# Opening of a graph-and-attention kernel: splitting the normalised input straight from PSUM

## What is computed

```python
x = x + gnn(layernorm(x), [src, dst], ...)      # two SAGE layers
x = x + ffn(layernorm(x), ...)                  # router, three attentions, MLP

def sage_conv(x, edge_index, W_l, b_l, W_r):
    src, dst = edge_index
    agg = segment_sum(x[src], dst) / max(segment_sum(1, dst), 1)[:, None]
    return agg @ W_l.T + b_l + x @ W_r.T
h = relu(sage_conv(x, edge_index, W1_l, b1, W1_r))
gnn = sage_conv(h, edge_index, W2_l, b2, W2_r)
```

## Time and profile before

| | us |
|---|---|
| median of 3 runs (lowest to highest) | 1723.16 (1722.98 to 1728.6) |
| the profiled execution, its time | 1724.62 |
| the profiled execution, its span | 1722.8 |
| PE busy | 1595.9 (93%) |
| DVE busy | 1140.0 (66%) |
| ACT busy | 872.8 (51%) |
| POOL busy | 744.8 (43%) |

### The profile page before, as it was taken

One profiled execution on the slowest core, in us unless ns is written; L12 is line 12 of the kernel. 1 busy time (PEld: TensorE's weight loads), 2 busy tenths in 40 slices (PEclk: granted clock), 3 DMA queues, 4 the chain that ended last, 5 costly groups with the idle time before them and its releaser, 6 DMA issues.

```text
span 1722.8 us, 26353 instructions
## 1 busy us (share of the span) xinstructions
PE 1595.9 (93%) x9714; PEld 1354.1 (79%) x9714; DVE 1140.0 (66%) x1810; ACT 872.8 (51%) x1733; POOL 744.8 (43%) x608
## 2 busy tenths in 40 slices
PE   2788999699999999999999998999999997899997
PEld 1467977588788888878789997878888885678876
DVE  7898735730788888840288885168898885843323
ACT  3796313321688878731177772158878872301100
POOL 3220222135436446133568773453545565632330
PEclk9999999799999999999999999999999998899999
DMA  3000011243021112042222304302111210110111
GB/s 101 18 26 2 26 55 55 83 178 72 8 54 31 31 31 56 7 184 69 60 60 61 71 9 150 90 1 57 34 31 31 73 49 19 38 37 25 49 37 59
DMA packets 37352, 91.62 MB, mean 53 GB/s; under 512 B 6462, under 2 KB 8980, under 8 KB 36717
## 3 DMA queue, kind: packets, MB, share of 16 engines
q1 hardware_dynamic: 37229, 89.99, 18.9%
HBM read 45.40 MB, written 13.86 MB: 34 GB/s over the span
## 4 chain that ended last, share of the span: by engine, by line
PE 78%; DVE 10%; ACT 6%; issue 3%; POOL 2%; DMA 1%; DVEq 0%; SPq 0%; ACTq 0%; POOLq 0%
PE ps L1088 14%; PE ps L1069 13%; PE ps L761 10%; PE ps L762 10%; PE ps L763 10%; PE ps L1054 8%; PE ps L1055 6%; ACT F L1355 1%; PE ps L1013 1%; PE ps L1014 1%; PE ps L1104 1%; ACT F L1364 1%; ACT F L1261 1%; PE ps L948 1%; ACT R L1274 1%
## 5 line engine op out<-in xcount | busy, mean ns | idle before, releaser
L1274 ACT ACTIVATE R<-ps 125x500 fp32r<-125x500 f32 (+3 forms) x632 | 291.7, 508 | 146.6 <-PE ps L1069 145.2
L1854 DVE TENSOR_REDUCE TB<-ps 125x1 f32<-125x1250 f32 (+4 forms) x240 | 299.5, 1262 | 82.1 <-PE ps L1055 56.5
L595 POOL TENSOR_TENSOR w_hi<-w_raw,zero 128x512 fp32r<-128x512 f32 x92 | 107.0, 1163 | 560.5 <-PE ps L763 281.5
L1863 DVE TENSOR_TENSOR R<-ps,R 125x500 fp32r<-125x500 f32 (+3 forms) x632 | 323.9, 568 | 12.9 <-ACT R L1274 12.9
L1261 ACT ACTIVATE F<-ps,TB 125x1250 f32<-125x1250 f32 (+4 forms) x240 | 275.9, 1156 | 60.2 <-DVE TB L1854 60.2
L1088 PE MATMUL ps<-R 125*128 125x252 f32 (+1 forms) x2080 | 288.9, 286 | 2.3 <-DVE F L1906 2.3
L1069 PE MATMUL ps<-ident,F 125*125 125x125 f32 x2040 | 260.0, 275 | 9.6 <-ACT F L1261 8.5
L1088 PEld LDWEIGHTS ps<-R 125*128 125x128 f32 x2080 | 256.1, 189 | 2.6 <-DVE R L1863 1.6
L1069 PEld LDWEIGHTS ps<-ident,F 125*125 125x125 f32 x2040 | 239.5, 189 | 13.1 <-ACT F L1261 12.7
L1054 PE MATMUL ps<-R 128*125 128x512 f32 (+5 forms) x624 | 240.1, 385 | 4.9 <-DVE R L1863 3.8
L761 PE MATMUL ps<-R,w_hi 128*128 128x512 f32 (+3 forms) x576 | 212.8, 370 | 17.8 <-POOL w_lo L610 11.2
(11 more groups left out here) (209 smaller groups left out, 2418.3 us busy)
## 6 DMA issues: line engine op xcount, KB each, us to landing
R<-F SPq DMA_DIRECT2D x96, 312.5 KB, 5.3
w_raw<-in_weights SPq DMA_DIRECT2D x88, 256.0 KB, 2.6
F<-in_weights SPq DMA_DIRECT2D x3, 1024.0 KB, 8.4
x_d<-F SPq DMA_DIRECT2D x10, 250.0 KB
zt_d<-F SPq DMA_DIRECT2D x1, 2500.0 KB, 14.0
F<-zt_d SPq DMA_DIRECT2D x1, 2500.0 KB, 9.2
xt_d<-F SPq DMA_DIRECT2D x4, 625.0 KB, 3.1
qc_d<-F SPq DMA_DIRECT2D x4, 625.0 KB, 5.6
```

The lines of the kernel that those rows point to most:

```text
L595: return eng.tensor_tensor(to, a, zero[0:to.shape[0], :].to_broadcast(list(to.shape)), ALU.add)
L1274: eng.activation(probs_run(K, n, 0, part, lo, hi), ps[0:P, 3 * (n % 2) + bank, P * (lo - j0):P * (hi - j0)] .rearrange("p (c t) -> p c t", ...
L1854: ins = eng.tensor_reduce(out=ngm[0:P, 2 * (n % 2) + part:2 * (n % 2) + part + 1], in_=flat(n % 2)[0:P, at:at + P * blocks], op=ALU.max, a ...
L1863: eng.tensor_tensor(probs_run(K, n, 1, part, lo, hi), ps[0:P, 3 * (n % 2) + bank, P * (lo - j0):P * (hi - j0)] .rearrange("p (c t) -> p c ...
```

## The change

- ACT copies each transposed tile from PSUM straight into the high part of `X0` (125 columns of each of the four blocks), and DVE subtracts it from PSUM straight into the low part, tile by tile, inside the normalising loop. The copy to `ZT`, `cut_hi` and `cut_lo` of `x` go, and with them the semaphore `sp["x"].lo`. `ln0.ev`, which frees the PSUM bank, is now counted up by DVE. PE waits for all ten tiles after its first group of the graph loop.
- The tile number of a source node is computed with three instructions (scale and shift, add 1.5 * 2^23, subtract it again, which rounds) in place of nine.
- POOL waits for these before it zeroes the 7580 columns, and zeroes the other 5120 in two halves, of which the first waits for the first five tiles. DVE waits for `at_zero` (now 4) ahead of its first `add_group`, no longer ahead of the loop.
- SP loads the weight units 0 and 1 behind `x` and ahead of the write at L474, units 2 and 3 behind the bias row, and then the five small constants.
- ACT runs one square root on a constant ahead of its first work.

```diff
--- before.py
+++ after.py
@@ -36,6 +36,7 @@
 WK = WD * NT
 TA = T + WD
 LAG = 2
+ROUND = 1.5 * 2 ** 23
 EPS = 1e-5
 SCALE = float(HD) ** -0.5
 BANK = 512
@@ -243,6 +244,7 @@
         mr1 = sb("mr1", [128, NT, 2])
         rcnt = sb("rcnt", [128, NT, 1])
         rt = sb("rt", [128, 48])
+        spare = rt[:, 6:7]
         b1g = rt[:, 40:44]
         bq_add = rt[:, 44:48]
         eps_t = sb("eps_t", [128, 1])
@@ -392,7 +394,7 @@
         comp = Sems(sem, "comp", "in_ row hi lo ps ev st")
         deg = Sems(sem, "deg", "lk sum ps free inv mem")
         sp = {n: Sems(sem, "cut_" + n, names) for n, names in
-              dict(x="hi lo", h="hi lo", s="val hi lo", os="hi lo", t="val hi lo st0 st1", ot="hi lo", oc="hi lo",
+              dict(x="hi", h="hi lo", s="val hi lo", os="hi lo", t="val hi lo st0 st1", ot="hi lo", oc="hi lo",
                    m="hi lo").items()}
         pj = {n: Sems(sem, "prod_" + n, names) for n, names in
               dict(g="ps a v", qk="a", v="ps v", u="a v t", uc="ps v", m1="a v t", m2="ps a v").items()}
@@ -464,12 +466,7 @@
             eng.dma_start(d_i, dst.rearrange("(q r) -> q r", q=EQ)).then_inc(e.in_, 16)
             for n, (lo, hi) in enumerate(X_LOADS):
                 eng.dma_start(XA[0:P, lo:hi, :], x[lo:hi, :, :].rearrange("i p f -> p i f")).then_inc(x_in[n], 16)
-            eng.dma_start(lncol[:], ln_cols[:, 0:6, :]).then_inc(small_in, 16)
-            eng.dma_start(b1g, ln_cols[:, 6, :]).then_inc(small_in, 16)
-            eng.dma_start(b1col[:], mlp_b1).then_inc(small_in, 16)
-            eng.dma_start(rt[:, 0:1], router_b1).then_inc(small_in, 16)
-            eng.dma_start(rt[0:1, 8:16], router_b2).then_inc(small_in, 16)
-
+            load_units(0, 2, G0)
             eng.wait_ge(e.mm, 2)
             eng.dma_start(mm_d.rearrange("m (q j) -> q m j", j=EJ), mm2.rearrange("q (m j) -> q m j", m=2)
                           ).then_inc(e.mmd, 16)
@@ -477,7 +474,13 @@
             for m in range(2):
                 eng.dma_start(dbc[:, m, 0:EC], mm_d[m:m + 1, :].to_broadcast([P, EC])).then_inc(e.mmi, 16)
             load_row(0, ROWB["g2"])
-            load_units(0, 16, G0)
+            load_units(2, 2, G0 + 2)
+            eng.dma_start(lncol[:], ln_cols[:, 0:6, :]).then_inc(small_in, 16)
+            eng.dma_start(b1g, ln_cols[:, 6, :]).then_inc(small_in, 16)
+            eng.dma_start(b1col[:], mlp_b1).then_inc(small_in, 16)
+            eng.dma_start(rt[:, 0:1], router_b1).then_inc(small_in, 16)
+            eng.dma_start(rt[0:1, 8:16], router_b2).then_inc(small_in, 16)
+            load_units(4, 12, G0 + 4)
             eng.wait_ge(deg.inv, 3)
             eng.dma_start(deg_d.rearrange("i p -> (i p)").unsqueeze(0), RB[0:1, :]).then_inc(deg.mem, 16)
             eng.wait_ge(deg.mem, 16)
@@ -587,6 +590,7 @@
             eng.memset(keyT[:, EC:EP], -1.0).then_inc(const_ok, 1)
             eng.memset(dbc[:, 0, EC:EP], float(T)).then_inc(const_ok, 1)
             eng.memset(dbc[:, 1, EC:EP], -1.0).then_inc(const_ok, 1)
+            eng.wait_ge(e.lk, 5)
             eng.memset(F[0:P, 5120:NT * TA], 0.0).then_inc(at_zero, 1)
             eng.memset(ones_sq, 1.0).then_inc(at_zero, 1)
 
@@ -717,8 +721,9 @@
 
             eng.wait_ge(const_ok, 12)
             cut_units(0, 4)
-            eng.wait_ge(ln0.tr, NT + 2)
-            eng.memset(F[0:P, 0:5120], 0.0).then_inc(at_zero, 1)
+            for lo, hi in ((0, HG), (HG, NT)):
+                eng.wait_ge(ln0.tr, hi + 2)
+                eng.memset(F[0:P, D * lo:D * hi], 0.0).then_inc(at_zero, 1)
             cut_units(4, 8)
             eng.wait_ge(deg.sum, 3)
             cut_units(8, UNIT["qs"])
@@ -1148,9 +1153,11 @@
                 turn(ln0, i % 2, i, XA[0:P, i, :])
             for g in range(NG):
                 group(g)
+                if g == 0:
+                    eng.wait_ge(ln0.ev, NT + 2)
                 i, k = g // KC, g % KC
                 if i < NT:
-                    product_part(pj["g"], i, k, UNIT["g1l"], X0, pj["g"].v, ready=sp["x"].lo)
+                    product_part(pj["g"], i, k, UNIT["g1l"], X0, pj["g"].v)
                     continue
                 done = [(g + d - KC * NT) * KC * NPC // (NG - 1 - KC * NT) for d in range(2)]
                 for n in range(done[0], min(done[1], KC * NPC)):
@@ -1307,6 +1314,7 @@
                                    ).then_inc(ce.hi, 1)
 
 
+            eng.activation(spare, zero[:], ACT.Sqrt)
             eng.wait_ge(e.tr, 1)
             for bank, t in ((4, loT), (5, keyT)):
                 eng.activation(t[:, 0:EC].rearrange("p (q j) -> p j q", j=EJ),
@@ -1315,9 +1323,10 @@
                 if i < NT:
                     deviation(ln0, i % 2, i)
                 if i:
-                    cols_out(ln0, (i - 1) % 2, i - 1)
-            eng.wait_ge(ln0.ev, NT + 2)
-            cut_hi(sp["x"], lambda k: ZT[:, k, :], X0, False)
+                    eng.wait_ge(ln0.tr, i + 2)
+                    eng.activation(X0[0][:, :, P * i - P:P * i],
+                                   ps[:, 6 + (i - 1) % 2, 0:KC * P].rearrange("p (k t) -> p k t", k=KC), ACT.Copy
+                                   ).then_inc(sp["x"].hi, 1)
             def rows_hi(J, n0, first_i=0, end_i=NT, at=bank_of):
                 for i in range(first_i, end_i):
                     eng.wait_ge(J.ps, n0 + i + 1)
@@ -1366,7 +1375,6 @@
                                bias=ones[0:P, 0:1], scale=-1.0).then_inc(lo_ready, 1)
 
             eng.wait_ge(const_ok, 12)
-            eng.wait_ge(sp["x"].lo, KC)
             squares(0)
             for g in range(NG):
                 if g + 1 < NG:
@@ -1487,9 +1495,9 @@
             eng.tensor_copy(d_f, d_i).then_inc(e.lk, 1)
             link.n = 2
             eng.wait_ge(e.lk, 2)
-            link(eng.tensor_scalar(h_f, s_f, float(P), None, ALU.is_ge))
-            for j in range(2, NT):
-                link(eng.scalar_tensor_tensor(out=h_f, in0=s_f, scalar=float(P * j), in1=h_f, op0=ALU.is_ge, op1=ALU.add))
+            link(eng.tensor_scalar(h_f, s_f, 1.0 / P, 0.5 / P - 0.5, ALU.mult, ALU.add))
+            link(eng.tensor_scalar(h_f, h_f, ROUND, None, ALU.add))
+            link(eng.tensor_scalar(h_f, h_f, ROUND, None, ALU.subtract))
             link(eng.scalar_tensor_tensor(out=l_f, in0=h_f, scalar=float(P), in1=s_f, op0=ALU.mult, op1=ALU.subtract))
             eng.scalar_tensor_tensor(out=k_f, in0=d_f, scalar=float(NT), in1=h_f, op0=ALU.mult, op1=ALU.add
                                      ).then_inc(e.mm, 1)
@@ -1506,18 +1514,23 @@
                 eng.bn_aggr(mv[0:P, b, :], stats[0:P, b, :]).then_inc(L.var, 1)
 
             c = Chain(eng, ln0.lk)
-            for i in range(NT + 1):
+            for i in range(NT + 2):
                 if i < NT:
                     for n, (lo, hi) in enumerate(X_LOADS):
                         if i == lo:
                             eng.wait_ge(x_in[n], 16)
                     stat(ln0, i % 2, XA[0:P, i, :], c)
-                if i:
+                if 1 <= i <= NT:
                     b = (i - 1) % 2
                     eng.wait_ge(ln0.std, i)
                     c(eng.reciprocal(sd[0:P, b, 1:2], sd[0:P, b, 0:1]))
                     eng.tensor_scalar(XA[0:P, i - 1, :], XA[0:P, i - 1, :], mv[0:P, b, 0:1], sd[0:P, b, 1:2],
                                       ALU.subtract, ALU.mult).then_inc(ln0.nrm, 1)
+                if i >= 2:
+                    tk = slice(P * (i - 2), P * (i - 1))
+                    eng.wait_ge(sp["x"].hi, i - 1)
+                    eng.tensor_tensor(X0[1][:, :, tk], ps[:, 6 + i % 2, 0:KC * P].rearrange("p (k t) -> p k t", k=KC),
+                                      X0[0][:, :, tk].bitcast(F32), ALU.subtract).then_inc(ln0.ev, 1)
 
 
             eng.wait_ge(const_ok, 12)
@@ -1541,11 +1554,6 @@
             eng.tensor_scalar(flags[:, 0:1], top[:, 0:1], 1.0, None, ALU.mult).then_inc(e.flags, 1)
             eng.tensor_scalar(flags[:, 1:2], top[:, 1:2], 1.0, None, ALU.mult).then_inc(e.flags, 1)
 
-            def cut_lo(S, get, X):
-                for k in range(KC):
-                    eng.wait_ge(S.hi, k + 1)
-                    eng.tensor_tensor(X[1][:, k, :], get(k), X[0][:, k, :].bitcast(F32), ALU.subtract).then_inc(S.lo, 1)
-
             def cut_affine(S, w, b, X, stored=False):
 
                 for k in range(KC):
@@ -1564,8 +1572,6 @@
                 eng.tensor_tensor(X[1][:, k, :], PB[:, k % 2, :], X[0][:, k, :].bitcast(F32), ALU.subtract
                                   ).then_inc(S.lo, 1)
 
-            eng.wait_ge(ln0.ev, NT + 2)
-            cut_lo(sp["x"], lambda k: ZT[:, k, :], X0)
 
             def rows_lo(J, a0, first_i=0, end_i=NT, at=bank_of):
                 for i in range(first_i, end_i):
@@ -1699,8 +1705,6 @@
                 eng.sem_inc(at_done, 1)
 
             eng.wait_ge(e.base, 5)
-            eng.wait_ge(sp["x"].lo, KC)
-            eng.wait_ge(at_zero, 3)
             def ends(n):
 
```

(2 more changed lines are left out.)

## The result

The changed kernel takes 1722.18 us (median of 22 runs, 1718.44 to 1723.75); the kernel before, measured beside it, takes 1724.8 (22 runs, 1722.98 to 1729.05). The ratio is 0.9982 with a 95% interval of 0.9975 to 0.9988: faster by about 3 us, half of the forecast 6. The profiled execution has a time of 1722.15 and a span of 1720.3, against 1722.8 before.

The account below looks back on a forecast made before the run. The opening was taken as bound by DVE, with the gain made at PE's first group: 47.7 - 53.66 = -6.0 us, so the median 1723.16 becomes 1717.2. The range was 1713.5 to 1721.5.

Parts of the forecast that it names:

- PE's first group: Start of PE's graph loop, at 53.66 before, forecast at 47.7; everything behind it was taken to shift equally.
- the 8 us: Opening on DVE: cheaper index numbers let tile 0's statistics begin near 8 instead of 16.08; x leaves some 2.
- Turns: DVE's normalising loop: each tile's turn grows from 1.56 to 2.16 by a low part from PSUM of 0.60.
- the bases: DVE's 15 instructions for the groups ahead of the graph loop, forecast to begin at 40.0 and end at 46.7.
- the splits of units 0 and 1: POOL's weight splits during the normalising loop, forecast to hold DVE for 0 to 4 us, taken as 1.6.
- the price of the bases: DVE's time for the bases ahead of the graph loop, forecast at 6.7, between 4.4 and 8.9.
- nothing held and held as before: The two ends for DVE's bases: 4.4 us without holding by POOL, 8.9 with holding as before.
- rival 2: Bases held as before or more by two splits and two memsets; first group at 49.8 to 51, 1720, chance 0.23.
- the page's rule: GpSimd contends with two-SBUF-input VectorE instructions, memsets not excepted; bases would end nearer to 48.9.
- The side that I argued away: At the bases, the zero memsets at 42.8 to 47.2 would hold DVE's subtraction, ending the bases nearer to 48.9.
- Rival 4: Behind the graph loop's start: it begins 6 earlier, but the gain misses the end; 1722.5, chance 0.03.
- The chances by 0.5%: Whole kernel against a 0.5% (8.6 us) threshold: faster 0.18, slower 0.03, within 0.79.

Follow-up runs that it names:

- e5: Changed kernel with the nine-step tile numbers put back and POOL's 7580-column memset no longer waiting; 1723.52 us, ratio to before 0.9991.
- e8: Changed kernel with ACT zeroing the 5120 columns and each x transfer issued as rows 0 to 119 and 120 to 124; 1711.21 us, ratio to before 0.9911.
- e1: Changed kernel with POOL starting the two halves of the zeroes only after DVE finished the bases; 1720.67 us, ratio to before 0.9962.
- e3: Changed kernel with ACT, not POOL, zeroing the 5120 columns tile by tile; 1719.52 us, ratio to before 0.9964.
- e7: Changed kernel with the copy to ZT restored and high and low parts made at once, the low behind the bases; 1723.54 us, ratio to before 0.9982.
- e4: Changed kernel with each transfer of x issued as rows 0 to 119 and rows 120 to 124; 1715.66 us, ratio to before 0.9937.

## Why the prediction was right or wrong

**What held.** PE's first group was the place to look at. The first cast takes 0.36, the numbers end at 8.0, tile 0 begins 0.5 behind them, and the 8 us shrink because of `x`: tile 2 at 14.46 (forecast 14.4), tile 5 at 25.27 (24.5). Turns are 2.15 (2.16). The last low part begins at 39.17, 1.8 behind the end of its normalise (37.36). The read-back is issued at 26.96 (26.7), unit 2 is split at 38.32 (37.9), the zeroes end at 47.38 (47.2). DVE comes to the bases at 39.76 (40.0), and that this fits so well is luck: tile 5 was 0.8 late, and the splits of units 0 and 1 held only about 0.6 in the loop where I took 1.6. Of the 8 us of faster numbers I left some 2 at tile 5. It came 1.0 earlier than before (25.27 against 26.24), and by e5 the numbers are worth 0.3 at the bases and 0.0 at the first group.

**What failed: the price of the bases.** I took 6.7, the middle between nothing held and held as before; they took 9.5: 4.1 by themselves (as in e8), 1.8 held by splits (0.94 for 0.21 and 1.60 for 0.50) and 3.6 by the memsets (3.91 for 0.34). With the memsets out of the way they took 6.1 and 5.6 (e1, e3). This is 2.8 of the 3.5 us between the gain that was forecast (6.0) and that of the profiled executions (2.5). The step that failed was to take the middle between two ends where the schedule itself could have decided. What the runs show in its place: a memset holds a `tensor_scalar` until it ends, and a second one queued behind it holds the same instruction on (3.91, 4.41, 2.60). The row for this stood in the profile of before: the cast of 4.64 had ended 0.35 after a memset of 6.40. I used it for the cast, and not for the bases, where the memsets were to run at 42.8 to 47.2 by my own schedule and the bases from 40.0. Had I placed the fifteen instructions against that interval, the first `tensor_scalar` of a kind that a memset holds would have had to wait for 47.2, and the bases would have ended near 48.7. That is rival 2, with its start of 49.8 to 51; it had 0.23.

**The rule weighed against the rows.** I set the page's rule against the rows and read the rows rightly: a subtraction with two SBUF inputs goes on beside a memset (e7's low parts until 48.68), and is held by a split (1.10 for 0.23). The Trainium skill has this exception on another page, SBUF - State Buffer, "SBUF: two separate sides": two SBUF inputs conflict only with a GpSimd instruction that reads SBUF; the rows agree. But the weighing settled nothing about the bases, because eight of the fifteen are `tensor_scalar`, and a memset does hold those of L1548 here and of L1542 in e4 (L1543 there), though not L1547 (0.35 at 43.43). The side that I argued away on the subtraction came true by the other kind of instruction.

**What the forecast left out.** The shift of the first group isn't that of the end. Rival 4 had 0.03, because I found nothing for it in the trace. But the two instructions that meet at 337 us, 0.11 apart, were such a thing: whoever shifts a chain by microseconds can turn such a pair around. It took 1.55, the clock gave some 0.5 back, and 2.5 were left at the end.

**The baseline.** The absolute number was 5.0 too low. 1.6 of it is the start from the median of three runs, 1723.16, where 22 runs give 1724.8; the profiled execution, 1724.62, was nearer. The rest is 2.4 at the first group (2.8 of the bases, less what came earlier in the loop and the one-hots), and 1.0 behind it.

The chances by 0.5% put 0.79 on "within", and the measured 0.18% lies there. The range ended at 1721.5, 0.7 below the measured 1722.18; neither a baseline 1.6 higher nor 1.5 us of give-back were in it.

## What to carry to other kernels

When work moves on POOL, write down the interval in which each of its instructions will run and lay DVE's instructions against it by kind: in these runs a cast or a `tensor_scalar` over many contiguous SBUF columns that started inside a memset waited for its end, and mostly for the end of the next one queued behind it. Make an early engine faster only after asking when its data come; here 7.6 us were worth nothing at the first group while `x` came as it did, and no tile waited for `x` once the rows of a transfer were cut as 120 + 5 and not 125. When parts of a change are undone one at a time and don't add up to the whole, look for two paths that ended together. And a shift at the start is a forecast for the end only if no two instructions further on meet on a shared port within a few tenths of a us.
